# Graph network kernel: the first layer's scatter-adds go to two copies of the table instead of four

## The reference, cut to what matters

```
head, tail = x[src], x[dst]
att  = sigmoid(concat(head, relation[type]) @ att_w + att_b)      # depends on (src, type) alone
aggr = segment_sum(att * tail, src, 6250)
x    = layernorm(x + tanh(aggr @ W.T + b))
```

## Time and profile before

| What | us |
|---|---|
| Median of three runs | 14073.66 |
| Lowest, highest of them | 14048.91, 14075.56 |
| Span of the profiled execution, first to last instruction | 14084.2 |
| From the first to the last scatter-add of the first layer | 188.5 to 1663.0 |
| POOL busy, whole span | 7724.8 (55%) |
| DVE busy, whole span | 7042.7 (50%) |
| PE busy, whole span | 6814.7 (48%) |

### The profile page before, as it was taken

One profiled execution on the slowest core, in us unless ns is written; L12 is line 12 of the kernel. 1 busy time (PEld: TensorE's weight loads), 2 busy tenths in 40 slices (PEclk: granted clock), 3 DMA queues, 4 the chain that ended last, 5 costly groups with the idle time before them and its releaser, 6 DMA issues. The chain is left out here.

```text
span 14084.2 us, 100376 instructions
## 1 busy us (share of the span) xinstructions
PE 6814.7 (48%) x27637; PEld 5669.8 (40%) x27637; DVE 7042.7 (50%) x12322; ACT 5152.3 (37%) x5609; POOL 7724.8 (55%) x7576
## 2 busy tenths in 40 slices
PE   5443366657756774777577646661111322232222
PEld 5433355545545553655455535551111211121111
DVE  5333345434444443444444546663444466646666
ACT  0011144444434443444344424442222243423432
POOL 7888755544444445344444455546665555545553
PEclk7555577768777776887677767775555565556555
DMA  5333322212211221122133323333332344434442
GB/s 154 36 36 33 58 51 58 56 39 55 54 49 42 56 55 42 48 55 55 40 90 91 86 72 97 97 89 89 115 109 96 116 143 136 140 94 141 138 140 81
DMA packets 782270, 1137.56 MB, mean 81 GB/s; under 512 B 500471, under 2 KB 559955, under 8 KB 774499
## 3 DMA queue, kind: packets, MB, share of 16 engines
q0 software_dynamic: 355008, 370.44, 14.1%
q1 hardware_dynamic: 363245, 417.03, 9.6%
q10 hardware_dynamic: 63926, 349.09, 6.2%
HBM read 680.14 MB, written 468.70 MB: 82 GB/s over the span
## 5 line engine op out<-in xcount | busy, mean ns | idle before, releaser
L970 POOL DMA_INDIRECT turned<-d_t,idx x5788 | 5465.9, 944 | 5006.3 <-DVE wide L1426 3228.1
L1115 PE MATMUL banks<-pair,hot 128*128 128x462 f32 x16184 | 3981.1, 402 | 1677.0 <-issue 1661.2
L1115 PEld LDWEIGHTS banks<-pair,hot 128*128 128x128 f32 x16184 | 3357.4, 208 | 2299.7 <-issue 1921.1
L1236 DVE TENSOR_TENSOR wide<-banks,member 128x462 f32<-128x462 f32 x1156 | 689.9, 634 | 2788.3 <-remote 2123.6
L1084 ACT COPY wide<-wide 128x952 f32<-128x952 f32 (+2 forms) x252 | 503.4, 1997 | 2831.5 <-DVE wide L1446 2800.7
L650 POOL DMA_INDIRECT d_acc<-work,idx x784 | 1237.7, 1579 | 263.9 <-issue 234.4
L733 ACT ACTIVATE hot<-keys,row 128x1024 fp32r<-128x1024 f32 (+1 forms) x1036 | 1073.1, 1117 | 277.9 <-PE banks L1115 204.9
L1171 PE MATMUL banks<-ident,wide 128*128 128x128 f32 x588 | 163.1, 423 | 1814.2 <-issue 945.2
L1446 DVE TENSOR_TENSOR_SCAN wide<-banks,wide 128x224 f32<-128x224 f32 (+4 forms) x1288 | 1036.9, 871 | 5.8
L1128 PE MATMUL banks<-pair,hot 128*128 128x448 f32 x3136 | 804.7, 417 | 452.1 <-issue 393.8
L1128 PEld LDWEIGHTS banks<-pair,hot 128*128 128x128 f32 x3136 | 688.1, 221 | 568.7 <-issue 492.5
(11 more groups left out here) (311 smaller groups left out, 9556.1 us busy)
## 6 DMA issues: line engine op xcount, KB each, us to landing
d_e<-wide ACTq DMA_DIRECT2D x168, 924.0 KB
turned<-d_t,idx POOLq DMA_INDIRECT x5788
d_e<-wide ACTq DMA_DIRECT2D x84, 1008.0 KB
wide<-d_b SPq DMA_DIRECT2D x60, 1344.0 KB
keys<-d_key SPq DMA_DIRECT2D x124, 512.0 KB
d_b<-wide SPq DMA_DIRECT2D x28, 1344.0 KB
wide<-d_edge SPq DMA_DIRECT2D x84, 448.0 KB
d_em<-wide ACTq DMA_DIRECT2D x84, 448.0 KB
```

The costliest lines, as they stand in the source:

```text
L970: gp.indirect_dma_start(rows[:, b, k, :], None, table[:, :], offset(idx[:, b, k:k + 1])).then_inc(s["gathered"][b], 16)
L1115: mm = nc.tensor.matmul(ps_cols[i], hot[:, place, i, j, :], flat(g.pair[:, part, j]), start=(j, part) == (0, 0), stop=(j, part) == (SETS - ...
L1236: nc.vector.tensor_tensor(found[:, i - i0], ps_cols[i].rearrange("p (w c) -> p w c", c=SET), mid(member[:, i], TW), ALU.mult).then_inc(pic ...
```

## The change

`REP` goes from 4 to 2. Everything that is counted by it follows: two tables `d_acc` are zeroed, column `k` goes to copy `k % 2`, the wait before it is for the scatter two places earlier, four primes and semaphores fewer, half the loads of sums in the next phase, and one level less in the tree of additions.

```diff
-REP = 4
+REP = 2
...
-                   "b_loaded spread_done added0 added1 added2 added3 idx_ready pairs_used")
+                   "b_loaded spread_done added0 added1 idx_ready pairs_used")
...
-    added = list(zip(s["added0"], s["added1"], s["added2"], s["added3"]))
+    added = list(zip(s["added0"], s["added1"]))
...
                 sums = part[:, j % BUFS]
-                link(nc.vector.tensor_tensor(sums[:, :, 0:2], sums[:, :, 0:2], sums[:, :, 2:4], ALU.add))
                 link(nc.vector.tensor_tensor(sums[:, :, 0], sums[:, :, 0], sums[:, :, 1], ALU.add))
```

## The result

| | Before | After |
|---|---|---|
| Median of the runs, us | 14074.61 | 14223.41 |
| Lowest, highest | 14048.91, 14085.67 | 14218.82, 14249.86 |
| Ratio, 95% interval | | 1.0114 (1.010 to 1.0129) |
| Span of the profiled execution | 14084.2 | 14220.7 |
| First to last scatter-add | 1474.5 | 1641.6 |

The change makes the kernel slower by 149 us (medians), where +110 and 14184 were forecast.

What follows compares the result with a forecast made beforehand. POOL's scatter-adds were taken as the bound: 1556 + 28 + 8.5 = 1593 us against 1475, so +118, less 8 in the node phase, +110. Forecast 14184 us (+0.78%), range 14125 to 14250.

Steps and rivals of the forecast that it cites:

- What bounds the kernel: Scatter-add stretch: POOL alone bounds it, 784 steps of 1.86 us, 1475 us together with slow descriptor work.
- How long a scatter holds its copy: Scatter-adds at L650: 3.19 us from a scatter's start to a waiter's start, read from ACT and POOL's queue.
- What a release costs: POOL, from the wait's end to the scatter-add's start: 0.78 us, with 0.27 and 0.91 as ends.
- Part 1: Scatter-add stretch: two chains of 392 with period 3.97 us, above the allowance of 3.72; 1556 us.
- Part 2: Scatter-adds landing late after each chunk's load of `b_rows`: 1.0 x 28 = 28 us, ends 0 and 31.
- Part 3: Scatter-add stretch: of 17 us of slow descriptor work half is left, 8.5 us.
- Part 4: Before the scatter-adds: fewer zeros and four primes fewer gain 0.
- Part 5: Node phase, fewer loads and additions of sums: -8 us, between -4 and -13, including 4 from later groups.
- A: Rival at the scatter-adds: release hidden, only slow landings show, 24 us at most; +16, 14090 us; chance 0.08.
- B: Rival at the scatter-adds: two copies are enough, only the lighter node phase shows; 14063 us; chance 0.05.
- D: Rival before the scatter-adds: zeroing is on the path, another -20 besides no scatter-add loss; 14043 us; chance 0.02.
- C: Rival at the scatter-adds: release costs 0.91 us through register work, period 4.10; +161, 14235 us; chance 0.13.

Runs made afterwards that it cites:

- experiment 11: Kernel before (four tables), each scatter-add waiting for the one just before it; stretch from first to last scatter-add 3171.2 us, kernel 15785.7 us.
- experiment 3: Changed kernel with POOL's loop written out, waits on constants and no counter step; scatter-add stretch 1544.6 us, ratio 1.0057 to the kernel before.
- experiment 7: Changed kernel with POOL's loop written out and waits on constants, counter step kept; scatter-add stretch 1642.9 us, kernel 14058.04 us in one run.
- experiment 4: Changed kernel without the loop's loads of `b_rows`, one load ahead instead (sums wrong); scatter-add stretch 1581.7 us, total 10635.22 us in one run.
- experiment 5: Changed kernel run again unaltered; 14059.54 against 13888.80 us for the kernel before, ratio 1.0125, scatter-add stretch 1642.7 us.
- experiment 1: Kernel before (four tables), each scatter-add waiting for the one two places earlier; scatter-add stretch 1650.4 us, 10701.10 against 10532.03 us, ratio 1.0162.
- experiment 8: Changed kernel with constant waits, no counter step and each `b_rows` load cut into four DMAs; scatter-add stretch 1517.4 us, ratio 1.0030 to kernel before.
- experiment 12: Changed kernel with constant waits, no counter step and each `b_rows` load held back by twelve counter steps; scatter-add stretch 1518.9 us, ratio 1.0025.
- experiment 2: Kernel before with only two of four tables loaded and added in the node phase (sums incomplete); 10525.02 against 10532.03 us, ratio 0.9992.

## Why the prediction was right, point by point

- *What bounds the kernel.* Right. POOL's 784 scatter-adds end last in this stage, and each of the 167 us is on the path: the first scatter of the node phase is 162.6 us later (1864.92 against 1702.33).
- *How long a scatter holds its copy*, 3.19 us. Right: 3.2 in the changed kernel, 3.26 in experiment 11. Taking it from those who wait for the DMA, ACT and POOL's queue, was enough.
- *What a release costs*, 0.78 between 0.27 and 0.91. Right: 0.74. The choice between the two forms of wait decided more than half of the loss, and experiments 3 and 7 show that it is the form: without the counter step 97 us are gone, with constants alone none. It did not decide the sign: with a release of 0.27 two tables still cost 60 us (10592.42 against 10532.03).
- *Part 1*, period 3.97, some +98 us for the steps. Measured: median distance of two back 3.963, so 1.982 a step against 1.861, and 783 x 0.121 = +94 us.
- *Part 2, slow landings*, 28 us with the ends 0 and 31. This term was mis-sized: experiment 4 gives 60 us, twice as much and outside its ends. The 4.3 was read at the fifth place of a chunk, where it stayed (4.4); the fourth place went from 3.6 to 5.8. The failed step is that a landing seen beside a transfer was taken for a constant, when it depends on which of the two comes first by half a microsecond, and the change itself moves that.
- *Part 3*, slow descriptor work half as visible, -8.5. No experiment measures it alone. An estimate: the two chains worked through scatter-add by scatter-add, each with its own duration, landing and release from the changed kernel's trace, give 1640.9 us for the stretch (1641.6 measured), and 1626.5 with all durations at 1.556. So 14 of the 17 us are still there, and the term was nearer -3.
- *Not in the forecast:* 14 slow releases, 13 of 2.1 us and one of 1.5 (last section), 13 x 1.36 + 0.8 = 18 us; the same estimate gives 18. Together 94 + 60 - 3 + 18 = 169, against 167.1 measured.
- *Part 4*, nothing from zeros and primes. Right: the first scatter-add came at 189.1 instead of 188.53.
- *Part 5, node phase*, -8 between -4 and -13. It gave -5.1: of its three pieces the loads and the first addition stood, the 4 us over the later groups did not come. The step that failed is that ACT would turn the sums earlier; PE's order holds them back.
- *Rivals.* A is what experiment 3 builds: with the release hidden the stretch was 1544.6, more than A's 24 us because of the loads. B and D fell with the 1641.6 us. C's 0.91 was not seen: its 14235 lies nearer to the measured median than the forecast does, but by coincidence, since its period of 4.10 is not there (3.963). The Trainium skill's fixed 2.0 us plus bytes ("DMA: Bandwidth & Descriptors", "Anatomy of one DMA — SWDGE (gpsimd) path"), under which nothing would have been lost, gives an estimated 2.1 us for what the traces show as 3.2 from the start, of which 1.56 is descriptor work; the 0.74 of the release comes on top between two uses of a table.

The range held, but the forecast time lay 39 us below the median. By the profile it was 162.6 - 110 = 53 us short: 32 from part 2, 18 from the slow releases, 6 from part 3 and 3 from the node phase, less 4 by which part 1 was too high; the 2 us over are within these readings. The period of the two chains was foreseen, the rest was luck in part: the terms that were off nearly all lay on one side, and they stayed inside the range because its high end had been drawn for another reason, C's longer release. The repeat in experiment 5, +171 us, would have landed near 14245, close under the upper end of 14250.

## What to carry to other kernels

A ring of buffers or tables is deep enough when depth x step is above landing plus release, with the release counted from the wait's end to the start of the next user; as long as it is deep enough none of these numbers is visible, so they have to be read from others who wait. Leave room for the worst landing, the one behind a big transfer, and not for the median: here 3.72 us were 0.2 short of the median and 2.6 short of the worst; at three places, 5.58, the stretch was back at 1480, because with steps of 1.86 nearly all landings beside a load, too, were back below 4.6 after a start. A counter step between wait and DMA cost 97 us over 784 scatter-adds with two tables; with four, the idle time of 0.30 shows nothing of it.

## What was not expected of the hardware

**Slow releases at regular places.** In the changed kernel 14 releases take 1.5 to 2.1 us instead of 0.74, while the landing is normal. (Others that look late in the trace only stand behind a delayed scatter-add.) They fall on scatter-adds 47, 75, 120, 128, 231, 239, 343, 351, 455, 463, 567, 575, 679 and 687 (the first is 0), which from 231 on are two series with 112 between members. One of them, 239, in the timeline, and its wait alone (697 to 698 us):

```profile
699.28 1.55 POOL L650 DMA_INDIRECT d_acc<-work,idx  x1 [1.67 <-DMA d_acc<-work,idx]
...
L649 POOLq EVENT_SEMAPHORE  x1: 17/17/17, 697.2 to 697.2; - x1
```

The wait passed at 697.2 and the scatter-add started at 699.28. The same places show without the loads (experiment 4) and with the loop written out (experiment 7); in experiment 1 they lie two earlier (229, 237), again 112 apart. So the loads and the form of the loop don't make them. But they do hang on the counter step: without it (experiments 3, 8 and 12) the idle time before scatter-add 120 and all later ones of the list is the usual 0.30, and only 47 and 75 still show 0.6 to 0.95. So the 97 us of experiment 3 hold most of these 18 us too. What happens there was not tried.

**The same kernel at 10532 and at 14084 us.** The kernel before took 14074.61 us in the runs of the result and 10532.03, 13888.80 and 14084.21 in the three sets of experiments, each within 0.3% in itself. The largest group of products over the whole execution, in the kernel before (first profile) and in experiment 2 (first set), with its busy time, the mean of one in ns, and PE's idle time before it:

```profile
L1115 PE MATMUL banks<-pair,hot 128*128 128x462 f32 x16184 | 3981.1, 402 | 1677.0 <-issue 1661.2
...
L1115 PE MATMUL banks<-pair,hot 128*128 128x462 f32 x16184 | 3473.5, 375 | 187.0 <-DVE wide L1236 140.1
```

The mean granted clock is 0.677 in the one and 0.749 in the other, but that is the smaller part. Of the 3560 us between the two profiled executions 508 are in the time of these products and 1490 in PE's idle time before them, put down to "issue", for which the profile shows no cause. Whether the clock is low because PE stands idle, or both come from something else, stays open. The scatter-adds, which PE does not bound, took the same in both. A loss in a POOL-bound stage is therefore a larger share where the rest of the kernel is faster: 169 us are 1.6% there and 1.1 to 1.2% elsewhere. The first and the third set were run on a chip of the same number, so the number of the chip alone does not decide it.
